# Two batches' third context tiles projected on spare rows of fourteen others, in an attention and mixture-of-experts kernel

## What is computed

```
# attention, per batch
q = layernorm(x) @ Wq.T            # 100 x 512
k_raw = context @ Wk.T             # 361 x 512
v_raw = context @ Wv.T             # 361 x 512
kv = concatenate([k_raw, v_raw], -1).reshape(b, m, 32, 16, 2)
k, v = kv[..., 0], kv[..., 1]
q, k = rmsnorm(q), rmsnorm(k)      # over the 16 elements of a head
x = x + tanh(g_xattn) * softmax(q @ k.T * 16**-0.5) @ v
# feed-forward
x = x + tanh(g_ffn) * (top-1 routed expert + shared expert)(layernorm(x))
```

## Time and profile before

| | |
|---|---|
| median of three runs | 958.12 us |
| the profiled execution | 960.27 us |
| its span | 958.2 us |
| TensorE busy | 939.0 us (98%) |
| VectorE, ScalarE, GpSimd busy | 620.5, 550.3 and 173.5 us |
| granted TensorE clock, mean | 0.994 |
| transfers | 129.98 MB, mean 136 GB/s |

### The profile page before, as it was taken

One profiled execution on the slowest core, in us unless ns is written; L12 is line 12 of the kernel. 1 busy time (PEld: TensorE's weight loads), 2 busy tenths in 40 slices (PEclk: granted clock), 3 DMA queues, 4 the chain that ended last, 5 costly groups with the idle time before them and its releaser, 6 DMA issues. The chain is left out here.

```text
span 958.2 us, 24714 instructions
## 1 busy us (share of the span) xinstructions
PE 939.0 (98%) x10503; PEld 784.9 (82%) x10503; DVE 620.5 (65%) x1446; ACT 550.3 (57%) x829; POOL 173.5 (18%) x206
## 2 busy tenths in 40 slices
PE   8899989999999999999999999999999999999997
PEld 6677767777777777777888999989888888888886
DVE  6766754867549566677686444443577777777774
ACT  5577766777676778767732211212356666666653
POOL 2001221211212221123243100001011122112111
PEclk9899999999999999999999999999999999999999
DMA  8554455564546755347563210103486787677762
GB/s 307 131 93 94 102 93 105 112 114 103 94 99 144 161 82 106 87 90 146 119 156 101 73 44 23 45 23 92 134 246 218 229 242 233 222 231 236 228 205 63
DMA packets 175627, 129.98 MB, mean 136 GB/s; under 512 B 114706, under 2 KB 151698, under 8 KB 175512
## 3 DMA queue, kind: packets, MB, share of 16 engines
q1 hardware_dynamic: 165800, 108.07, 45.6%
q0 software_dynamic: 6544, 16.46, 5.6%
q10 hardware_dynamic: 3168, 3.81, 1.2%
HBM read 88.79 MB, written 13.56 MB: 107 GB/s over the span
## 5 line engine op out<-in xcount | busy, mean ns | idle before, releaser
L644 PE MATMUL bank<-arena_f32r 128*128 128x512 f32 (+1 forms) x1272 | 322.2, 403 | 6.4 <-DVE arena_f32r L1025 4.7
L644 PEld LDWEIGHTS bank<-arena_f32r 128*128 128x128 f32 (+1 forms) x1272 | 225.4, 184 | 69.1 <-DVE arena_f32r L1025 7.0
L851 ACT ACTIVATE probs<-score_banks 128x2000 f32<-128x2000 f32 (+1 forms) x80 | 142.1, 1776 | 55.4 <-PE score_banks L664 55.1
L1739 PE MATMUL bank<-xnT,arena_f32r 128*128 128x224 f32 (+1 forms) x756 | 109.8, 296 | 0.7 <-DVE arena_f32r L1695 0.7
L1800 ACT ACTIVATE hT_hi<-arena_f 128x224 fp32r<-128x224 f32 (+2 forms) x96 | 42.2, 441 | 116.1 <-DVE arena_f L1811 109.9
L1739 PEld LDWEIGHTS bank<-xnT,arena_f32r 128*128 128x128 f32 x756 | 103.2, 190 | 3.2 <-DVE arena_f32r L1695 1.2
L1044 DVE TENSOR_REDUCE sumsq<-arena_f 128x32 f32<-128x512 f32 (+2 forms) x61 | 41.6, 682 | 67.0 <-ACT arena_f L807 67.0
L1811 DVE TENSOR_TENSOR arena_f<-bank,arena_f 128x224 f32<-128x224 f32 (+2 forms) x93 | 41.2, 443 | 66.8 <-PE bank L1739 66.3
L681 PEld LDWEIGHTS bank<-probs,values 128*17 128x17 f32 (+1 forms) x3072 | 64.1, 97 | 17.8 <-issue 17.5
L681 PE MATMUL bank<-probs,values 128*17 128x100 f32 (+1 forms) x3072 | 76.0, 250 | 0.8 <-issue 0.8
L1695 DVE TENSOR_TENSOR arena_f32r<-arena_f,arena_f32r 128x1024 fp32r<-128x1024 f32 x43 | 52.6, 1224 | 13.8 <-ACT arena_f32r L1688 13.5
(11 more groups left out here) (247 smaller groups left out, 1792.8 us busy)
## 6 DMA issues: line engine op xcount, KB each, us to landing
arena_f<-L_ffn_w_gate_up SPq DMA_DIRECT2D x48, 512.0 KB
arena_f<-L_ffn_w_down SPq DMA_DIRECT2D x24, 512.0 KB
arena_f<-ctx SPq DMA_DIRECT2D x15, 722.0 KB, 5.8
w_raw<-L_ffn_w_gate_up SPq DMA_DIRECT2D x16, 512.0 KB
w_raw<-L_ffn_w_down SPq DMA_DIRECT2D x8, 512.0 KB
x_all<-x SPq DMA_DIRECT2D x8, 400.0 KB
x_rows<-x_all SPq DMA_DIRECT2D x4, 800.0 KB
x_all<-x_rows POOLq DMA_DIRECT2D x4, 768.0 KB, 6.7
```

The lines of the kernel that those rows point to most:

```text
L644: product = PE.matmul(bank[0:rows, :], src[:, j, 0:rows], weight, start=(m == 0), stop=(m == 11))
L851: A.activation(k.probs[n % 2][:, :, 0:blocks, :], k.score_banks[:, :, 0:blocks * k.N].rearrange("p j (r n) -> p j r n", r=blocks), ACT.Exp ...
L1739: made = PE.matmul(bank[:, 0:width], weight[a][:, i, :], xs[x][:, i, 0:width], start=(i == 0 and n == 0), stop=(i == k.KD - 1 and n == 2))
```

## The change

- **Spread tiles.** Batches 7 and 15 don't project a third tile any more. Their 105 last context rows are cut into seven pieces of 16 (the last of 9), and each piece is put, in the input as laid out for the kernel, into rows 112 to 127 of the third tile of another batch: 0 to 6 carry for 7, 8 to 14 for 15. These 14 third tiles have 128 rows now, of which 0 to 104 are their own. After the pack and the values of such a tile are made, `sp_share_tail` puts the 16 columns of keys (a transposing DMA of 32 rows) and the 16 rows of values (a plain DMA) into `spread_kT` and `spread_values`, in slot 33 of the preparation. Scores and weighted values of batches 7 and 15 read their third tile there; batch 8's piece waits until batch 7 is done with the buffers.
- **Plan.** Batches 7 and 15 have 60 products, spread over the same 24 slots, 2.5 a slot, with both keys ahead of both values.
- **Context by tiles.** Each tile is a transfer of its own (L1576) into a ring of four buffers, loaded four tiles ahead.
- **Third pack buffer.** `k_pack[t]`: a pack waits for its own tile's turn of the batch before (tile 2 for the sharing turn too).
- **Outputs.** The first half of a batch's outputs is taken one slot later (slot 15, where it was 14), but in the last batch.
- The small sums and roots move from buffers of their own into the arena, whose size and order are changed; GpSimd clears the third pack buffer too.

```diff
+SPREAD = {7: (0, 1, 2, 3, 4, 5, 6), 15: (8, 9, 10, 11, 12, 13, 14)}
+SHARE = 16
+SPREAD_PLAN = Plan(tiles=LATER_PLAN.tiles,
+                   projections=((KEYS, 3), (KEYS, 0), (KEYS, 1), (VALUES, 0), (VALUES, 1), (KEYS, 2), (VALUES, 2)),
...
+SHARE_SLOT = 33
+CONTEXT_TILES = 4
...
-        k.ctx_raw = [carve(P, [KD * k.M], F32) for _ in range(2)]
+        k.ctx_raw = [carve(P, [KD * P], F32) for _ in range(CONTEXT_TILES)]
...
-        k.k_pack = [buf(f"k_pack{t}", [P, H, HW], F16) for t in range(2)]
+        k.k_pack = [buf(f"k_pack{t}", [P, H, HW], F16) for t in range(k.NMT)]
...
+        k.spread_values = buf("spread_values", [P, H, HD + 1], F32)
+        k.spread_kT = buf("spread_kT", [P, H // GH, HW - SHARE + SHARE * len(SPREAD[7])], F16)
...
 def tiles_of(b):
-    return [t for t in plan(b).tiles if t != QUERIES or query_tile(b) is not None]
+    return [t for t in plan(b).tiles if (t != QUERIES or query_tile(b) is not None) and (t != 2 or b not in SPREAD)]
...
+    if b in SPREAD:
+        return n * 24 // 60
     return (n - 12) * 10 // 24 if n < 36 and query_tile(b) is None else n * 24 // 84
...
     for t in sorted({t for _, (_, t) in blocks_of(u)}):
-        w.wait_ge(k.pack_turned[t], 16 * (b + 1))
+        if t in tiles_of(b):
+            w.wait_ge(k.pack_turned[t], 16 * (b + 1 - (without_tails(b) if t == 2 else 0)))
+        else:
+            w.wait_ge(k.shared_keys, 16 * shares_for(b))
...
     for r, (_, (block, t)) in enumerate(blocks_of(u)):
+        keys = k.kT[b % 2][:, block, P * t:P * t + P] if t in tiles_of(b) else k.spread_kT[:, block, HW - SHARE:HW - SHARE + k.M - P * t]
...
-                if i == pv_slot(k, b, half_units(z) - 1) + 1:
+                if i == pv_slot(k, b, half_units(z) - 1) + (2 if z == 0 and b < k.B - 1 else 1):
                     act_take_outputs(k, A, w, b, z)
...
-        w.wait_ge(k.pack_turned[(2, 1, 0)[t]], 16 * (b + (t == 2)))
+        w.wait_ge(k.pack_turned[t], 16 * (b - (without_tails(b) if t == 2 else 0)))
+        if t == 2:
+            w.wait_ge(k.shared_keys, 16 * shares_to(b - 1))
...
-def sp_load_context(k, SP, w, b):
-    if b >= 2:
-        w.wait_ge(k.src_low, tiles_to(b - 2, 2))
-    SP.dma_start(k.ctx_raw[b % 2], k.ctxT[b]).then_inc(k.ctx_in[b % 2], 16)
+def sp_load_context(k, SP, w, n):
+
+    b, t = k.contexts[n]
+    if n >= CONTEXT_TILES:
+        w.wait_ge(k.src_low, tiles_to(*k.contexts[n - CONTEXT_TILES]))
+    load_context_tile(k, SP, b, t)
...
+def sp_share_tail(k, SP, w, b):
+
+
+    to, i = share_of(b)
+    w.wait_ge(k.pack_low, packs_to(b, 2))
+    w.wait_ge(k.v_copied, contexts_to(b, 2))
+    if shares_for(to - 1):
+        earlier = max(before for before in SPREAD if before < to)
+        w.wait_ge(k.scored, UNITS * earlier + UNITS)
+        w.wait_ge(k.weighted, UNITS * earlier + UNITS)
+    w.wait_ge(k.shared_keys, 16 * shares_to(b - 1))
+    first = SHARE * (len(SPREAD[to]) - 1 - i)
+    SP.dma_start(k.spread_kT[:, :, first:first + HW], k.k_pack[2][P - HW:P].rearrange("p h c -> p (h c)"),
+                 transpose=True).then_inc(k.shared_keys, 16)
+    SP.dma_start(k.spread_values[first:first + SHARE], k.values[b % 2][P - SHARE:P, 2]).then_inc(k.shared_values, 16)
...
-            if j == source_slot(b, 2) + 2 and b + 2 < k.B:
-                sp_load_context(k, SP, w, b + 2)
+                if t < k.NMT and j == source_slot(b, t) + 2:
+                    n = k.contexts.index((b, t)) + CONTEXT_TILES
+                    if n < len(k.contexts):
+                        sp_load_context(k, SP, w, n)
+            if share_of(b) and j == SHARE_SLOT:
+                sp_share_tail(k, SP, w, b)
...
+    k.rows_of = lambda t, b: ((P if share_of(b) else min(P, k.M - P * t)) if t < k.NMT
+                              else min(P, k.T - P * query_tile(b)))
```

119 lines of the change are left out of this document (74 added, 45 removed).

## The result

The changed kernel takes **951.82 us** (median of 6 runs, 949.43 to 952.99), the kernel before 957.95 (6 runs beside it, 956.33 to 961.47). The ratio is 0.9931, 95% interval [0.9913, 0.9949]: 6.1 us faster where 15.0 were forecast, and just outside the range of 940.0 to 950.5. The profiled execution took 952.10 us for its span of 949.8.

What follows compares the result with a forecast made beforehand. TensorE was taken to bound the kernel, busy 939.0 of 958.2 us. From the median 958.12, -11.0 - 4.1 - 0.7 + 0.8 = -15.0 us gave 943.1 us, range 940 to 950.5.

Steps and rivals of the forecast that it cites:

- Part 1: Key and value projections of batches 7 and 15: 48 products fewer at 0.230 us each, -11.0 us.
- Part 2: Third tiles of 14 batches, 128 rows for 105: longer weight loads lie beside the products, 0 us.
- rival c: Wider third tiles: weight loads show instead of being hidden, +6.7 us, total 949.8; chance 0.05.
- Part 3: Batch 3's start: a third pack buffer ends ScalarE's wait and the TensorE stop behind it, -4.1 us (0 to 4.1).
- Part 4: Unit at 312.97 us: copying outputs later brings the source's high part 0.71 us earlier, -0.7 us (0 to 1.4).
- Part 5: Two stretches preparing batches 7 and 15, with 2.5 projections a slot: +0.4 us each, +0.8 us; bounds 0 and 8.2.
- Part 6: New turns, row copies and context loads by tile: covered by slack before their use, 0 us.
- a: A TensorE stop like batch 3's remains or comes anew: 4.1 us, total 947.2; chance 0.20.
- b: Thin stretches: ScalarE paces them, waiting replaces the removed products and their whole gain is lost, 954.1 us; chance 0.06.
- d: SyncE's queue in the 14 carrying batches: new turns cause stops of 4.1 us each, 967.7 us with six; chance 0.03.

Runs made afterwards that it cites:

- two_packs: The changed kernel with two key pack buffers, the third tile's pack in the first tile's as before; 951.16 us, ratio 0.9940.
- no_spread: The changed kernel with no batch spread, all 16 batches projecting their third tile, the rest kept; 953.37 us, ratio 0.9958.

## Why the prediction was wrong

- **Part 1, 48 products, -11.0.** The price holds: where nothing waits, units with five products fewer are 1.16 to 1.18 us shorter (6.1, 6.2; 14.1), those with four 0.92 to 0.99. The sentence "All of it is on the engine that bounds the stage" failed: 8.1 us of it came back as stops in the two stretches and right behind them (-2.9 in place of -11.0). At 0.230 us for each missing product that is 2.4 us in units 6.0 to 7.0, 2.5 in 14.0 and 3.3 in 14.3.
- **Part 2, wider tiles, 0.** Right. In the carrying batches runs of 17 and 18 projections take what the earlier trace rows has:

```profile
317.27 4.38 PE L687 MATMUL bank<-arena_f32r 128*128 128x512 f32 x18
...
323.11 4.15 PE L687 MATMUL bank<-arena_f32r 128*128 128x512 f32 x17
```

  A weight load of 128 columns takes 188 ns in the mean on the page of the profile, had 189, and lies beside the products. So rival c, which charged it, is false. By the Trainium skill ("TensorE: Matmul & The Clock Gate", section "LDWEIGHTS") the load grows with the columns. The step from 105 to 128 agrees, 20 ns for 19. The level doesn't, 188 ns for the 107 of the prediction, and the measurement decides.
- **Part 3, pack buffer, -4.1.** Mechanism right, size off: -3.0 in the change's trace; two_packs has 3.6 more. The copy of the outputs behind it was next and waited 2.95 us for its turn; I had looked for the next thing late on VectorE alone, and named 0.3 us of it.
- **Part 4, outputs later, -0.7.** Right: measured -0.8 in unit 9.3, with a forecast of 0 to 1.4.
- **Part 5, thin stretches, +0.8.** The step that failed. "A source's high part has about 1 us in hand" was read from one place, and I priced the stretches by ScalarE's and VectorE's mean load of a batch. What decided was when single results are there: in batch 14's first unit a source's low part, behind other work of VectorE (2.20 us of stop), and in its fourth the first weights' low part, at the end of a chain over two engines that takes 7.7 us from the last keys, and took 7.2 with all products beside it (1.50 us of stop, and a clock of 0.56 behind it). The feed-forward weights' split behind that chain is not in the prediction at all. In these stretches and right behind them the stops cost 8.1 us in place of 0.8. That is the upper end (8.2) that I had set as "one stop with its clock as in 3 for each" and gave too little chance; that it agrees so well is luck, for it is made of five stops of other sizes.
- **Part 6, transfers, 0.** No one waited for the new turns themselves: there are 14, and the view of their line names nobody. My bound held for their issue (a median of 1.18 us, under 1.3) and was a little short for the landing (3.7 us, over 3.5):

```profile
L1636 SPq DMA_TRANSPOSE spread_kT<-k_pack x14: 1180/1184/1858, 45.3 to 431.1; - x14
...
DMA to landing us min/median/max: 2.4/3.7/5.7
```

  But the loads of context by tiles, which I passed over in a sentence on their distance to use, stand in SyncE's queue ahead of an outputs' turn and hold it; some 1.4 us in units 7.0 and 11.0.
- **Rivals.** a was what happened, with two long stops and three short ones rather than the one I allowed for. With two stops at 4.1 each it had 951.3, just outside the range, and the measured 951.82 is 0.5 from that. Its chance of 0.20 was for stops that remain or come anew singly, while the cause (less time for the same chain) applies to both stretches at once. b (ScalarE paces) has the right outcome for batch 15, all of its 5.5 us lost, but the wrong engine: ScalarE waited there too. d had the right queue; no run showed TensorE lose to the sharing turns, and without them (no_spread) ScalarE waits nearly as long for the outputs (17.1 us for 19.5).
- Terms as measured in the traces: -2.9, -3.0, -0.8, +0.5 (unit 11.0) and -0.6 in small pieces make the -6.8 between unit 0.1 and 15.1, of the medians' -6.1. The -8.2 between the two profiled executions has 1.45 more from unit 0.0, below.
